# A graph-attention and expert kernel: whole products in the first block of destinations, and work moved in its set-up and ahead of a branch

## The reference

```python
def _gat(x, src, dst, W, a_src, a_dst, b, heads, ch, concat):
    h = (x @ W).reshape(n, heads, ch)
    es = (h * a_src).sum(-1)
    ed = (h * a_dst).sum(-1)
    e = leaky_relu(es[src] + ed[dst], 0.2)
    w = exp(e - segment_max(e, dst)[dst])
    alpha = w / segment_sum(w, dst)[dst]
    out = segment_sum(h[src] * alpha[:, :, None], dst)
...
h = relu(layernorm(gat(layernorm(x), W1, 4 heads, 64 channels)))
x = x + gat(h, W2, 1 head, 256 channels)
x = x + moe(layernorm(x))      # top 2 of 8 experts, 256 -> 1024 -> 256
```

## Time and profile before

| | |
|---|---|
| median of 3 runs | 1428.64 us |
| lowest, highest | 1409.08, 1430.99 us |
| the profiled execution | 1437.54 us, its span 1435.5 us |
| mean granted TensorE clock in it | 0.896 |
| busy, share of the span | PE 85%, PEld 56%, DVE 59%, POOL 50%, ACT 49% |

### The profile page before, as it was taken

The page is one execution under the profiler, slowest core; times in us unless marked ns, Lnnn a source line. Parts: engine busy times, 40 slices in busy tenths (PEclk is TensorE's granted clock), DMA queues, the critical chain, the costliest instruction groups (busy, mean ns, idle before and its releaser), DMA issues.

```text
span 1435.5 us, 26517 instructions
## 1 busy us (share of the span) xinstructions
PE 1216.6 (85%) x8723; PEld 800.5 (56%) x8724; DVE 853.8 (59%) x2522; ACT 702.5 (49%) x1854; POOL 711.8 (50%) x621
## 2 busy tenths in 40 slices
PE   3789888888888988957787787794699999999997
PEld 3533333333333333335464565563699999999996
DVE  8677788888789979733565765786422222222221
ACT  3656566757577767833343343341434344334432
POOL 1000677676668874026665666640144445454544
PEclk9955798899999999968788899897799999999999
DMA  5232643643564382063544554544033332323221
GB/s 162 86 95 73 150 110 104 175 122 94 148 152 108 101 213 71 27 232 94 157 140 152 163 182 125 164 110 115 12 94 93 95 97 37 95 37 97 35 37 26
DMA packets 137158, 157.16 MB, mean 109 GB/s; under 512 B 58935, under 2 KB 116504, under 8 KB 137064
## 3 DMA queue, kind: packets, MB, share of 16 engines
q0 software_dynamic: 33616, 73.02, 21.5%
q1 hardware_dynamic: 102888, 82.42, 18.7%
q10 hardware_dynamic: 560, 0.52, 0.1%
HBM read 121.19 MB, written 35.52 MB: 109 GB/s over the span
## 4 chain that ended last, share of the span: by engine, by line
PE 50%; DVE 22%; issue 11%; ACT 5%; another core or an unknown queue 5%; DMA 4%; POOL 2%; DVEq 0%; POOLq 0%; SPq 0%; ACTq 0%
PE bank L1480 11%; PE bank L1488 11%; PE bank L1350 10%; PE bank L1431 6%; DVE ring_a L1958 4%; PE bank L1198 3%; ACT ring_a L1062 2%; DVE ohk L1700 2%; POOL arena L830 2%; DVE ring_a L2018 2%; DMA out_x<-ring_a,si 2%; PE bank L1401 1%; DVE st L1553 1%; DVE ohs L1696 1%
## 5 line engine op out<-in xcount | busy, mean ns | idle before, releaser
L830 POOL DMA_INDIRECT arena<-rows,idx_e x365 | 411.9, 1128 | 334.0 <-issue 90.6
L1350 PE MATMUL bank<-ring_a,slots 128*64 128x384 f32 (+1 forms) x2000 | 331.1, 518 | 44.6 <-DVE ring_a L1958 34.5
L1431 PE MATMUL bank<-h2t,ring_a 128*128 128x257 f32 x700 | 194.0, 423 | 29.5 <-DVE ring_a L2018 15.6
L1958 DVE SCALAR_TENSOR_TENSOR ring_a<-ring_a,arena 128x1536 f32<-128x1536 f32 (+1 forms) x125 | 192.6, 1541 | 41.9 <-ACT ring_a L1062 28.7
L1062 ACT ACTIVATE ring_a<-vbb,slots 128x384 f32<-128x384 f32 x400 | 212.2, 605 | 7.2 <-DMA vbb<-v_rows 4.1
L1170 ACT ACTIVATE ring_a<-bank,cols 128x128 f32<-128x128 f32 x432 | 129.0, 371 | 160.9 <-PE bank L1480 160.6
L1431 PEld LDWEIGHTS bank<-h2t,ring_a 128*128 128x128 f32 x700 | 141.4, 212 | 66.2 <-issue 29.1
L1350 PEld LDWEIGHTS bank<-ring_a,slots 128*64 128x64 f32 x2000 | 81.5, 136 | 133.0 <-issue 64.4
L876 POOL DMA_INDIRECT gs<-gates,gk x54 | 51.4, 951 | 149.3 <-DVE gk L2110 136.0
L1480 PEld LDWEIGHTS bank<-ring_a,arena 128*128 128x128 f32 x1056 | 123.1, 192 | 1.7
L1480 PE MATMUL bank<-ring_a,arena 128*128 128x128 f32 x1056 | 123.2, 275 | 0.0
(11 more groups left out here) (308 smaller groups left out, 1709.4 us busy)
## 6 DMA issues: line engine op xcount, KB each, us to landing
counts_all<-arena SPq DMA_DIRECT2D x14, 800.0 KB
arena<-counts_all SPq DMA_DIRECT2D x14, 800.0 KB
arena<-in_L_ffn_W SPq DMA_DIRECT2D x8, 1024.0 KB, 7.4
vbb<-v_pairs SPq DMA_DIRECT2D x23, 320.0 KB
arena<-rows,idx_e POOLq DMA_INDIRECT x365
XB<-general_sums SPq DMA_DIRECT2D x38, 130.0 KB
vbb<-in_L_ffn_W SPq DMA_DIRECT2D x4, 1024.0 KB
spare<-in_L_ffn_W SPq DMA_DIRECT2D x4, 1024.0 KB
```

Source lines behind the costliest of these rows:

```text
L830: pool.indirect_dma_start(to[:, k, 0:width], None, table, bass.IndirectOffsetOnAxis(idx_e[:, m * PAIR + k:m * PAIR + k + 1], 0)).then_inc( ...
L1350: ins = pe.matmul(to, weights, S1[q % SLOTS1][:, h * w_:(h + 1) * w_], start=(s == 0), stop=(s == NT - 1))
L1431: ins = pe.matmul(bank[(j % 2) * 2 + i][:, 0:W2T], S2[q2 % SLOTS2][:, i * P:(i + 1) * P], h2t[:, s, 0:W2T], start=(s == 0), stop=(s == NT ...
L1958: v.scalar_tensor_tensor(a, a, 1.0, C1[b][:, s, 0:k * P].unsqueeze(1).broadcast_to([P, HEADS, k * P]), ALU.max, ALU.mult).then_inc(s_a, 1)
```

## The change

**Block 0** takes one product for each head, of 65 weight columns (64 channels and the denominator), into a bank of its own: banks 0 to 3. `sums_out(0)` makes four copies of 65 partitions, and tile 0 is turned by four transposes. The visits in block 0 keep to banks 4 and 5 (N_EARLY).

**Set-up.** The keys are transposed at n = 19, and the first visits begin at n = 21: twelve ride in the loop, twelve follow the last projection. ACT takes the roots of chunks 1 to 3 at steps 5, 9 and 14 of its loop in place of 2, 6 and 11. DVE takes the statistics of chunk 2 and the scale of chunk 3 sooner, and puts `last_edges`, `unpack_pairs` and W2's `score_columns` behind all 24 one-hots.

**Second layer.** ACT, not DVE, negates p, and v is spread for the first block before the flag is loaded and the branch taken.

```diff
+KEYS_AT = 19
-N_EARLY = B1[0][1] * PER_TILE
+N_EARLY = N_FIRST // VISITS + len({w for q in range(NT + 1) for w, v, u in VISITS_AT.get(q, ()) if v == 0})
+        OT0 = spare[0:CH + 1, 0:HEADS * P]
...
-                if n + 1 in (2, 6, 11):
-                    chunk_root((2, 6, 11).index(n + 1) + 1)
+                if n + 1 in (5, 9, 14):
+                    chunk_root((5, 9, 14).index(n + 1) + 1)
...
-                if n == 12:
+                if n == KEYS_AT + 1:
                     keys_out(0)
...
+                if layer:
+                    act.wait_ge(s_ex, 4)
+                    act.activation(np2[:, :, :], p2[:, :, :], ACT.Copy, scale=-1.0).then_inc(s_ex, 1)
...
-                for i in range(PASSES):
+                for h in range(HEADS) if b == 0 else ():
+                    act.wait_ge(s_mm, (NT - 1) * PASSES + min(h + 1, PASSES))
+                    ins = act.activation(OT0[:, h * P:(h + 1) * P], bank[h][0:CH + 1, 0:P], ACT.Copy)
+                    if h != PASSES - 1:
+                        ins.then_inc(s_ot, 1)
+                for i in range(PASSES) if b else ():
...
             weights(1, p2, pu2[:, :, :], v2, np2[:, :, :], v2[:, :, :], SLOPE)
+            rows_out(B1[0][1])
             act.wait_ge(s_fl, 2)
...
-            act.wait_ge(s_vt, 2)
...
-                if n == 11:
+                if n == KEYS_AT:
                     keys_T(0)
...
+                    if t == 0:
+                        for h in range(HEADS):
+                            ins = pe.transpose(bank[6][:, h * (CH + 1):(h + 1) * (CH + 1)], OT0[:, h * P:(h + 1) * P], ident[0:CH + 1, 0:CH + 1])
+                        ins.then_inc(s_tr, 1)
+                        continue
...
-                        for h in range(2 * i, 2 * i + 2) if values else range(HEADS):
+                        for h in range(i, HEADS if i == PASSES - 1 else i + 1) if b == 0 else ():
+                            ins = pe.matmul(bank[h][0:CH + 1, 0:P], slots[:, s, h * (CH + 1):(h + 1) * (CH + 1)],
+                                            S1[q % SLOTS1][:, h * P:(h + 1) * P], start=(s == 0), stop=(s == NT - 1))
+                        for h in () if b == 0 else range(2 * i, 2 * i + 2) if values else range(HEADS):
...
             extremes(1, 1)
+            pe.wait_ge(s_ex, 3)
+            spread_rows(range(B2[0][0], B2[0][0] + B2[0][1]))
             pe.wait_ge(s_fl, 2)
...
             unpack()
+            chunk_refine(3)
+            ffn_columns()
+            v.wait_ge(s_lk, 1)
+            for u in range(N_FIRST):
+                onehots(*FIRST_VISITS[u], u)
             last_edges()
+            unpack_pairs()
             v.wait_ge(s_w, 16 * 7)
             score_columns(w2a, 1, 1)
-            ffn_columns()
-            chunk_refine(3)
-            v.wait_ge(s_lk, 1)
-            for u in range(N_FIRST):
-                if u == 4 * VISITS:
-                    unpack_pairs()
-                onehots(*FIRST_VISITS[u], u)
```

More of the change, by code:

```diff
@@ L952, in _ @@
                                    bank[(3, 7)[t % 2]][:, 0:D].rearrange("p (h c) -> p h c", c=CH), ACT.Copy).then_inc(s_HS, 1)
-                if n >= 14:
-                    while VISITS * (done + 1) <= 2 * (n - 13) and done < N_FIRST // VISITS:
+                if n >= KEYS_AT + 3:
+                    while VISITS * (done + 1) <= 2 * (n - KEYS_AT - 2) and done < N_FIRST // VISITS:
                         window_out(done)
@@ L1084, in _, with rows_out @@
                 q += 1
+            def rows_out(n):
+                act.wait_ge(s_vb, n + 1)
+                what = next((what for q, what in ROWS_AT.items() if ROWS_OF[q] == n), 0)
+                if isinstance(what, str):
+                    k = int(what[-1])
+                    m = len(EDGE_TILES[k * 4:k * 4 + 4]) * P
+                    act.activation(ve2[:, k * 512:k * 512 + m], bank[7][:, 0:m], ACT.Copy).then_inc(s_vbs, 1)
+                else:
+                    m = B2[what][1] * P
+                    act.activation(vb2[what % 2][:, 0:m], bank[7][:, 0:m], ACT.Copy).then_inc(s_vbs, 1)
             weights(1, p2, pu2[:, :, :], v2, np2[:, :, :], v2[:, :, :], SLOPE)
+            rows_out(B1[0][1])
             act.wait_ge(s_fl, 2)
@@ L1112, in hooks2 @@
                     act.activation(xnT[:, e % 4, :, :], bank[6][:, 0:D].rearrange("p (k n) -> p k n", k=2), ACT.Copy).then_inc(s_TS, 1)
[L1114 to L1123, removed]
             def exponents(p):
@@ L1229, in _ @@
                     pe.transpose(bank[5][:, 0:100], vecs[0:100, :], ident[0:100, 0:100]).then_inc(s_vecT, 1)
-                if n == 11:
+                if n == KEYS_AT:
                     keys_T(0)
-                if 13 <= n < 13 + N_FIRST // 2:
-                    if n == 13:
+                if n >= KEYS_AT + 2:
+                    if n == KEYS_AT + 2:
                         pe.wait_ge(s_vecT, 2)
-                    for u in (2 * (n - 13), 2 * (n - 13) + 1):
+                    for u in (2 * (n - KEYS_AT - 2), 2 * (n - KEYS_AT - 2) + 1):
                         visit(*FIRST_VISITS[u], u)
-            for u in range(2 * (NT + 2 - 13), N_FIRST):
+            for u in range(2 * (NT - KEYS_AT), N_FIRST):
                 visit(*FIRST_VISITS[u], u)
@@ L1365, in _, with spread_rows @@
                 q += 1
+            def spread_rows(tiles):
+                for i, t in enumerate(tiles):
+                    ins = pe.matmul(bank[7][:, i * P:(i + 1) * P], v2[:, t, 0:1].broadcast_to([P, P]), ident[:, :], start=True, stop=True)
+                ins.then_inc(s_vb, 1)
             pe.wait_ge(s_HS, 2 * NT)
@@ L1376, in _ @@
                 general_layer(1, 1, lambda s, h: h2t[:, s, 0:W2T], W2T)
-            def spread_rows(tiles):
-                for i, t in enumerate(tiles):
-                    ins = pe.matmul(bank[7][:, i * P:(i + 1) * P], v2[:, t, 0:1].broadcast_to([P, P]), ident[:, :], start=True, stop=True)
-                ins.then_inc(s_vb, 1)
             def rows_at(q):
@@ L1422, in _ @@
             pe.wait_ge(s_vt, 2)
-            spread_rows(range(B2[0][0], B2[0][0] + B2[0][1]))
             q2 = 0
@@ L1634, in _ @@
             chunk_refine(1)
+            chunk_stats(2)
             for k, (lo, hi) in enumerate(REACH):
@@ L1747, in tables @@
                 v.sem_inc(s_fl, 1)
-                v.wait_ge(s_ex, 2 * layer + 2)
-                if layer:
-                    link(v.tensor_scalar(npv[:, :, :], p[:, :, :], -1.0, None, ALU.mult))
+                if layer == 0:
+                    v.wait_ge(s_ex, 2)
                 return v.value_load(flags[0:1, layer:layer + 1], min_val=0, max_val=1)
```

3 lines of the change are left out of this document (1 added, 2 removed).

## The result

| | before | changed |
|---|---|---|
| median of 20 runs each, us | 1430.52 | 1410.45 |
| lowest and highest, us | 1409.08, 1443.45 | 1399.74, 1426.44 |
| profiled execution, us | 1437.54 | 1415.02 |

The ratio is 0.9894 with a 95% interval of 0.9868 to 0.992: some 1% faster, within the 2% that counts as no change. The forecast was 1406.0 for the median and 1414.9 for the profiled execution.

What follows compares the result with a forecast made beforehand. Block 0 was taken as bound by TensorE at its lower clock level, 2.93 us a step. Gains of 21.6 (block 0), 1.0 (set-up) and 0 (second layer), 22.6 together, off 1428.64 gave 1406.0 us, range 1396 to 1424.

Steps and rivals of the forecast that it cites:

- block 0: Block 0 with whole products: the clock level rises, DVE's 2.02 us a step sets the pace, 75.4 becomes 53.8, gaining 21.6 us.
- set-up: Before block 0: earlier roots and keys let the tables start sooner, gaining 1.0 us, with ends of -3 and +2.
- the stages behind: Blocks 1 to 4 and the rest should only move; a rival had them take back some 8 us (1414), chance 0.08.
- 24 steps of 2.02: Block 0's steps at DVE's pace, 48.5 us, before 5.3 for the end of the block with the hand-over.
- The size of the lower-level step: TensorE's step in block 0 without a clock rise: 2.78 us, 0.14 less than now, with visits unchanged at 1.07.
- the level stays: Rival: TensorE stays at 1.2 GHz in block 0, gaining 3.5 us there and 1424 in all, chance 0.10.
- Why the level rises: TensorE in block 0: full-width products one after the other, as in set-up, raise the clock level within the first steps.
- the lowest run of before: Left open: block 0 of that run, 21.9 us under the highest, may have had the upper clock level.
- last projection forecast at 55: TensorE in set-up: the last projection moves from about 65 to about 55 us.
- DVE's tail: DVE's work between the last one-hot and the tables in set-up: 7.5 us, from 57.5 to 65.0.
- The second layer: Second layer's start: ACT's first weights come about a microsecond sooner, lost in its wait for gathered rows; 0 gained, bounds 0 to 1.
- The gather wait in block 1: Early in block 1: if five gathers aren't there when the first pair is used, one wait of up to 3 us.

Runs made afterwards that it cites:

- e2_narrow: Changed kernel with the narrow side-by-side products, their copies and tile 0's transposes of before put back in block 0, visits on two banks: median 1367.4 us, ratio 1.0057.
- e9_hold2: e3_hold with 8, 2 and 9 unread products around set-up's end and 2 in step 0 of block 0, narrow products kept: median 1348.01 us, ratio 0.9904.
- e3_hold: Kernel before, block 0 untouched, with 28 unread full-width products on TensorE where it idles ahead of block 0: median 1368.94 us, ratio 1.001.
- e4_infill: e2_narrow with one more unread full-width product of 264 columns in each step of block 0: one run, 1357.15 us.
- e5_changed: The changed kernel, unaltered, run on the chip of e6_fill and e8_layer2: median 1407.22 us, ratio 0.9909 to the kernel before.
- e12_changed: The changed kernel, unaltered, run on the chip of e9_hold2 and e11_whole: median 1348.54 us, ratio 0.992 to the kernel before.
- e1_whole: Kernel before with the block-0 part alone (whole products, four sum copies, tile 0's transposes, two visit banks): median 1346.56 us, ratio 0.9862.
- e11_whole: e1_whole again, kernel before with the block-0 part alone, beside the changed kernel on one chip: median 1349.1 us, ratio 0.993.
- e8_layer2: Kernel before with the second layer's start alone changed (v spread ahead of the branch, negated exponents on ACT): one run, 1441.8 us.
- e6_fill: Changed kernel with W2's score columns and the last edges moved ahead of DVE's wait for the keys: median 1405.42 us, ratio 0.9874.

## Why the prediction was right, and where it wasn't

**The number.** The profiled execution came within 0.1 us of the 1414.9 forecast, and that is partly luck: block 0 brought 1.35 more than forecast, set-up 1.3 less, the stages behind gave back 0.4, and the time outside the span was 0.3 less. The median is 4.5 above its forecast of 1406.0, for before had a median of 1428.64 in three runs and 1430.52 in twenty, and fell by less than the profile did.

**Block 0.** Right in size: 21.6 forecast, 22.95 measured. DVE sets the pace at 2.02, as forecast. The missing 1.4 is the end of the block: I counted 24 steps of 2.02, but step 24 follows step 23 by some 0.6 (two instructions in 1.28 us at 123.74), as the scales end with step 22 and step 24 has no one-hots ahead of it. Where I put 0.5 for the last window's copy, DVE idles 0.31, and the profile names no releaser. The copies of tile 0 lie under DVE's work, and no visit waits for a window's copy. The transposes don't lie in block 0 but in block 1, where TensorE is full, and there the change brings something that I overlooked. Before, tile 0's turn to rows holds up TensorE from 160.67 to 163.55, with waits between its six instructions; now it takes 0.30:

```profile
160.67 0.47 PE L1312 MATMUL bank<-ident,spare 128*128 128x128 f32 x2
...
163.55 0.50 PE L1198 MATMUL bank<-ohk,ohs 128*128 128x400 bf16 x1 [0.55 <-issue]
```

```profile
136.96 0.46 PE L1322 MATMUL bank<-ident,spare 65*128 65x65 f32 x4
137.26 0.33 PE L1208 MATMUL bank<-ohk,ohs 128*128 128x400 bf16 x1
```

By DVE's first instruction of each block, block 1 is 2.5 us shorter (117.98 for 120.48); the stages behind give it back.

**The size of the lower-level step.** I had 2.78, and it is 2.45. The products were as forecast, so 65 columns of weights cost what 128 do; the visits were not as they are (1.07): they take 0.73, each some 0.11 less. It is their neighbours and not their banks: in e2_narrow, with the visits on two banks and narrow products around them, they take 0.44, 0.37 and 0.28 again. So the narrow products cost the visits time too, which I had put on the products alone. With a step of 2.45 the rival "the level stays" would have gained 25 x 0.47, some 12 us, not 3.5. The trace agrees here with the rule of the Trainium skill, TensorEngine Tiling (Array Packing), Key Properties, that changing the tiling mode drains TensorE.

**Why the level rises.** The outcome was right, and the reason half right. I took it that products one after the other raise the level and narrow ones side by side don't. In all seven profiles of kernels with whole products that began block 0 low it rose, 3.7 to 6.2 us behind DVE's first block instruction. In e9_hold2 the narrow products hold the upper level for all of block 0, and in e3_hold it rises under them after some 47 us. In e4_infill it rises 9 us into the block once a full-width product is added to each step. My reading, which fits these runs: narrow steps that begin low seldom lift the level, and narrow steps that begin high keep it. Why is open: nothing here shows what in the narrow step holds the level down. What the change brings is that block 0 leaves the lower level within some 6 us in every profile. The narrow step costs 1.79 at the upper level and the whole one 1.27, and both hide under DVE's 2.02: fewer passes are worth nothing in themselves there.

One more thing on my reading of set-up. I read its lower level (the products at 24.64) from their length, 0.88 us for each of 264 columns. PEclk shows 1.00 there, so the clock column and the lengths disagree in that stretch:

```profile
22.00:26.00 4.00, 1.84 (x6) 1.53 (x7) 3.22 (x23) 1.84 (x5) 0.00 (x0) 1.00 0.36 70
```

In block 0 they agree (0.43 us for a whole product of 128 columns at 0.50, which is the same time a column), and I go by the lengths.

**The runs of the kernel before.** I named it as open that the lowest run of before might have had the upper level. The two groups of e3_hold, 16 us apart, and the mean clocks of the runs of before speak for it; no profile of the unaltered kernel shows such a run. It would also explain why the median fell by 20.1 and not by 22.6 (and by 20.1 and 15.6 on the chips of e5_changed and e12_changed): the profiled execution of before had the lower level through all of block 0, and some of its other runs may not have had it.

**Set-up.** I forecast block 0 to begin 1.0 sooner, and it began 0.3 later in the one pair of profiles. The pairs on one chip don't agree: 0.6 later (e2_narrow against e1_whole), 0.8 sooner (e12_changed against e11_whole) and 1.9 sooner (e5_changed against e8_layer2). So a gain of 1.0 is neither shown nor ruled out, and the medians of e11_whole and e12_changed are 0.6 apart. The structure was right: last projection forecast at 55 and measured at 54.86, DVE's tail forecast at 7.5 and measured at 66.16 - 58.49 = 7.7. The last one-hots were at 58.1 in place of 57.5; fourteen visits, not twelve, followed the last projection. The tables' small products ran at the lower level after 8.46 us of idle time, and block 0 began 10.93 behind the memset, where before has 10.30; but e5_changed has 10.69 and e12_changed 10.62, so that it is these products isn't shown. e6_fill shows the bound from the other side: of DVE's 7.7 behind the one-hots 3.1 was taken away, and the memset came 3.2 sooner.

**The second layer and the rest.** 0 forecast and right, by the mechanism named (e8_layer2); the wait at the pair's exponents is 6.18 in the changed kernel, 1.5 longer, forecast 1. The gather wait in block 1 came once, 1.65 us on DVE at 137.42, ahead of the first pair's weights, as put (up to 3). The first gather led block 1 by 129.54 - 125.30 = 4.2 us, forecast 5.

## What to carry to other kernels

Where a stretch runs at the lower level with its engine "busy" throughout, ask first what keeps the clock there and what the engine does just ahead: here some twenty unread products ahead of the block and in its first step were worth as much as the rewritten products. Work taken off an engine pays only down to the next engine's pace, 2.02 here. A kernel whose runs spread over 1 to 2% may owe it to such a stretch, so look at each run's mean clock before judging a change by a single profile. And take the start of a stage from more than one profile before calling half a microsecond a gain: here it stood between 76.18 and 78.28 us in four profiles of one and the same set-up (e1_whole, before, e11_whole, e8_layer2).

## What the runs showed of the hardware

Adding a matrix product to each step (0.55 us at the upper level) shortened the step from 2.93 to 2.34 us once the level had risen (e4_infill, one run). TensorE's same step took 2.93 us from 81.76 to 129.37, some 15 times, and 1.81 afterwards with nothing changed in the program (e3_hold). A visit between narrow products took some 0.11 us longer at the lower level than one between whole products (0.44, 0.36 and 0.27 against 0.33, 0.24 and 0.16).

Block 0 takes the same time on all three chips (50.6 with whole products), but the whole kernel differs by 57 us: 1347.8 us of span in e12_changed against 1404.5 in e5_changed. Blocks 1 to 4 and the second layer, which gather rows from memory, are where it goes: DVE's first block instruction of the second layer is at 596.9 against 612.4, with block 0 ending at 127.6 and 127.1. From the first gather of the experts' stage to the end both take the same within a microsecond: 410.3 and 410.1. That the gathers are the cause isn't shown, and what differs between the chips wasn't tried.
